# Coefficient matmuls taken apart and begun ahead of the first lookup, in a recommendation tower on one NeuronCore

## The reference

```python
e = jnp.stack([tbl_0[ids[:, 0]], ..., tbl_15[ids[:, 15]]], axis=1)     # (2048, 16, 16)
A = jnp.repeat(x0, s, axis=1)                                          # x0: (2048, 39, 16)
Bm = jnp.repeat(xl, f, axis=2).reshape(b, s * f, d)                    # xl = e
z = jnp.einsum('bnh,bnd,nk,khd,kd->bkh', A, Bm, alpha, w, hv[..., 0])
h = jnp.concatenate([z.reshape(B, -1), dense_ctx], axis=1)             # 256 + 16
h = jnp.maximum(h @ W_top1 + b_top1, 0.0)                              # 512
h = jnp.maximum(h @ W_top2 + b_top2, 0.0)                              # 256
y = h @ W_top3
```

## Time and profile before

| what | value |
|---|---|
| median of 3 runs | 206.78 us (206.12 to 207.69) |
| profiled execution | 207.17 us, of it 205.4 us span of the core |
| PE busy | 171.9 us, 84% of the span |
| DVE busy | 149.0 us, 73% |
| ACT busy | 65.1 us, 32% |
| POOL busy | 113.2 us, 55% |
| mean granted TensorE clock | 0.95 of 2.4 GHz |

### The profile page before, as it was taken

One profiled execution on the slowest core, in us unless ns is written; L12 is line 12 of the kernel. 1 busy time (PEld: TensorE's weight loads), 2 busy tenths in 40 slices (PEclk: granted clock), 3 DMA queues, 4 the chain that ended last, 5 costly groups with the idle time before them and its releaser, 6 DMA issues.

```text
span 205.4 us, 5054 instructions
## 1 busy us (share of the span) xinstructions
PE 171.9 (84%) x2170; PEld 128.2 (62%) x2170; DVE 149.0 (73%) x171; ACT 65.1 (32%) x203; POOL 113.2 (55%) x119
## 2 busy tenths in 40 slices
PE   0318958998638899999967999999899899899983
PEld 0307947896425677677845677777577467477671
DVE  3798872109999979898899968866979595595000
ACT  2098000729300118216201271181117317311322
POOL 2687777777777777777777777777750000000000
PEclk9999995558996999999999999999999999999999
DMA  6495999999837992991039819800693790000000
GB/s 199 146 305 156 218 205 201 271 181 267 214 77 143 197 207 27 214 199 21 6 70 199 164 26 229 175 13 10 155 206 65 184 222 6 0 3 0 3 0 2
DMA packets 11698, 26.63 MB, mean 130 GB/s; under 512 B 3836, under 2 KB 6396, under 8 KB 9628
## 3 DMA queue, kind: packets, MB, share of 16 engines
q1 hardware_dynamic: 5356, 20.50, 45.2%
q10 hardware_dynamic: 2688, 4.76, 7.7%
q0 software_dynamic: 3632, 1.06, 4.6%
HBM read 26.26 MB, written 0.05 MB: 128 GB/s over the span
## 4 chain that ended last, share of the span: by engine, by line
PE 59%; DVE 26%; issue 9%; DMA 2%; ACT 1%; SPq 1%; ACTq 0%; DVEq 0%
DVE prod L576 14%; PE bank L667 13%; PE bank L688 13%; PE bank L698 12%; PE bank L627 10%; PE bank L610 4%; DVE picked L536 4%; DVE onehot L524 3%; PE bank L682 2%; PE bank L657 2%; DMA prod<-slot_mask 2%; PE bank L608 2%; DVE dense_sb L466 1%; DVE prod L498 1%; PE bank L707 1%
## 5 line engine op out<-in xcount | busy, mean ns | idle before, releaser
L322 POOL DMA_INDIRECT e_all<-tbl,ids_sb x112 | 111.7, 998 | 37.6 <-issue 33.8
L576 DVE TENSOR_TENSOR prod<-x_main,bank 128x2048 f32<-128x2048 f32 x32 | 72.2, 2279 | 17.9 <-PE bank L657 9.1
L667 PE MATMUL bank<-prod,coef 128*32 128x256 f32 x640 | 43.5, 391 | 9.0 <-DVE prod L576 8.9
L627 PE MATMUL bank<-parts,onehot 125*128 125x80 bf16 (+1 forms) x864 | 39.6, 211 | 11.6 <-DVE onehot L524 5.6
L627 PEld LDWEIGHTS bank<-parts,onehot 125*128 125x128 bf16 x864 | 37.3, 108 | 15.8 <-issue 6.0
L401 ACT ACTIVATE spread<-e_all 128x128 f32<-128x128 f32 (+3 forms) x128 | 29.0, 329 | 17.5 <-DVE e_all L540 17.2
L667 PEld LDWEIGHTS bank<-prod,coef 128*32 128x32 f32 x640 | 17.0, 110 | 23.4 <-DVE prod L576 12.7
L688 PE MATMUL bank<-z_sb,w1z_sb 128*128 128x256 f32 x128 | 30.3, 380 | 0.0
L698 PE MATMUL bank<-h_sb,w_sb 128*128 128x256 f32 x128 | 29.8, 386 | 0.7 <-ACT h_sb L411 0.7
L698 PEld LDWEIGHTS bank<-h_sb,w_sb 128*128 128x128 f32 x128 | 23.7, 190 | 6.9 <-ACT h_sb L411 3.1
L536 DVE TENSOR_TENSOR picked<-bank,pick 128x320 f32<-128x320 f32 (+1 forms) x36 | 16.7, 465 | 15.2 <-PE bank L627 15.1
(11 more groups left out here) (41 smaller groups left out, 77.2 us busy)
## 6 DMA issues: line engine op xcount, KB each, us to landing
x_main<-x_m SPq DMA_DIRECT2D x16, 512.0 KB
x_last<-x_l SPq DMA_DIRECT2D x8, 1024.0 KB
low_h<-low_dram ACTq DMA_DIRECT2D x6, 768.0 KB, 8.7
e_all<-tbl,ids_sb POOLq DMA_INDIRECT x112
x_last<-dense_t SPq DMA_DIRECT2D x8, 128.0 KB
prod<-small_tables SPq DMA_DIRECT2D x1, 672.0 KB, 4.6
w1z_sb<-w1z SPq DMA_DIRECT2D x1, 512.0 KB, 14.3
w_sb<-w SPq DMA_DIRECT2D x1, 512.0 KB, 14.3
```

What stands on the lines that cost most here:

```text
L322: pool.indirect_dma_start(out=e_all[:, t * E + s * D:t * E + (s + 1) * D], out_offset=None, in_=tables[s], in_offset=bass.IndirectOffsetOn ...
L576: dve.tensor_tensor(prod[:, c, :, :], x0[:, p, :, :], value_bank(g, c // 2)[:, c % 2 * GB:(c % 2 + 1) * GB].unsqueeze(1).broadcast_to([P, ...
L627: last = pe.matmul(look_ps[i % 2][:, t * w:(t + 1) * w], onehot[:, n, c, at:at + P], parts[:, part, col:col + w], start=(t == 0 and c == 0 ...
L667: last = pe.matmul(z_ps[p][32 * q:32 * q + 32, a * GB:(a + 1) * GB], coef[:, c, 4 * a + q, :], prod[:, c, 4 * a + q, :], start=(c == 0 and ...
```

## The change

PE: `make_coef` is taken apart into `main_coef` (four matmuls, into `c_ps`) and `last_coef` (one matmul, into `c4_ps`). Eight `main_coef` are issued ahead of the first lookup, one behind each lookup from n = 1 on, and two `last_coef` behind each lookup from n = 3 on; the last four `last_coef` stand behind the last lookup. `c_done` now counts to 2.

DVE: `multiply_weights` moves ahead of `spread_alpha`, and `make_pick` behind it. `split_dense` moves from behind the third product of group 0 to in front of the first. SP: the inputs of the coefficients go first and the small tables last; `low_h` is loaded on SP's queue and not on ACT's, the second set of it behind `x0` of group 1; dense and `w1d` are loaded ahead of `x0` of group 0. ACT: `round_dense` goes in front of `spread_group(0, 0)`.

```diff
-COEF_FROM, DENSE_AT = 3, 2
+COEF_FROM = 3
...
             sp.dma_start(ids_i, ids_d).then_inc(digits_in, 16)
-            sp.dma_start(table_sb, small_tables).then_inc(table_in, 16)
             sp.dma_start(masks_sb[:, :], masks).then_inc(masks_in, 16)
+            sp.dma_start(w_hv_sb[:, :], w_hv.unsqueeze(0).broadcast_to([J, D, K * H + K])).then_inc(coef_in, 16)
             sp.dma_start(alpha_sb[:, :, :], alpha.rearrange("(c p) k -> p c k", p=P)).then_inc(prep_in, 16)
             sp.dma_start(mask_sb, slot_mask).then_inc(prep_in, 16)
-
-            sp.dma_start(w_hv_sb[:, :], w_hv.unsqueeze(0).broadcast_to([J, D, K * H + K])).then_inc(coef_in, 16)
+            sp.dma_start(table_sb, small_tables).then_inc(table_in, 16)
+
+            def load_low(a, n, count):
+
+                sp.dma_start(low_h[:, n:n + count, :], low_dram[n:n + count, a * HALF:(a + 1) * HALF].unsqueeze(0).broadcast_to(
+                    [P, count, HALF])).then_inc(low_in[n // 3], 16)
+
+            sp.wait_ge(low_stored, 16)
+            for n in range(0, NSMALL, 3):
+                load_low(0, n, 3)
...
-            load_x0(0, 0)
             for q in range(4):
...
                 sp.dma_start(w1d_f[rows, :], w1d).then_inc(dense_in, 16)
+            load_x0(0, 0)
...
-            for g in range(1, GROUPS):
+            load_x0(1, 1)
+            sp.wait_ge(onehot_ready, 2 * NSMALL)
+            for n in range(0, NSMALL, 3):
+                load_low(1, n, 3)
+            for g in range(2, GROUPS):
                 load_x0(g, g % 2)
...
-                act.wait_ge(c_done, 1)
+                act.wait_ge(c_done, 2)
...
-            act.wait_ge(low_stored, 16)
-            for n in range(0, NSMALL, 3):
-                load_low(0, n, 3)
             spread_weights()
             spread_sums()
...
+            round_dense()
             act.wait_ge(pads_done, 1)
             spread_group(0, 0)
             copy_coef()
-            round_dense()
-            act.wait_ge(onehot_ready, 2 * NSMALL)
-            for n in range(0, NSMALL, 3):
-                load_low(1, n, 3)
...
+            multiply_weights()
+            spread_alpha()
             make_pick()
-            spread_alpha()
...
-            multiply_weights()
             split_tables(1, slice(FIRST_COLS, W))
...
+            split_dense()
             for i in units_at(0):
...
                     if g == 0 and c == 3:
-                        dve.wait_ge(c_done, 1)
+                        dve.wait_ge(c_done, 2)
...
-                    if g == 0 and c == DENSE_AT:
-                        split_dense()
...
+            sum_alpha()
+            pe.wait_ge(bsum_copied, 2)
+            pe.wait_ge(wblock_done, 1)
+            for k in range(K - NSMALL + 1):
+                main_coef(k)
+            pe.wait_ge(split_step, 4)
             made = 0
-            sum_alpha()
-            pe.wait_ge(split_step, 4)
             for n in range(NSMALL):
                 if n == 3:
                     pe.wait_ge(split_step, 8)
                 look_up(n)
+                if n > 0:
+                    main_coef(K - NSMALL + n)
+                if n == COEF_FROM:
+                    pe.wait_ge(blast_done, 1)
                 if n >= COEF_FROM:
-                    make_coef(made)
-                    made += 1
+                    for k in range(made, made + 2):
+                        last_coef(k)
+                    made += 2
             for k in range(made, K):
-                make_coef(k)
+                last_coef(k)
```

More of the change, by code:

```diff
@@ L328, in _ @@
         def _(act):
-            def load_low(a, n, count):
-                act.dma_start(low_h[:, n:n + count, :], low_dram[n:n + count, a * HALF:(a + 1) * HALF].unsqueeze(0).broadcast_to(
-                    [P, count, HALF])).then_inc(low_in[n // 3], 16)
             act.wait_ge(warm_ready, 1)
@@ L597, in sum_alpha, with main_coef @@
                 last.then_inc(bsum_done, 1)
-            def make_coef(k):
-                if k == 0:
-                    pe.wait_ge(bsum_copied, 2)
-                    pe.wait_ge(wblock_done, 1)
-                    pe.wait_ge(blast_done, 1)
+            def main_coef(k):
                 for j in range(2):
@@ L607, in make_coef, with last_coef @@
                         row = 64 * j + 32 * odd
-                        pe.matmul(c_ps[row:row + FM, k * MC * HP:(k + 1) * MC * HP], bsum_sb[:, 0:FM, k],
-                                  wblock[:, k, j::2, odd::2], start=True, stop=True)
+                        last = pe.matmul(c_ps[row:row + FM, k * MC * HP:(k + 1) * MC * HP], bsum_sb[:, 0:FM, k],
+                                         wblock[:, k, j::2, odd::2], start=True, stop=True)
+                if k == K - 1:
+                    last.then_inc(c_done, 1)
+            def last_coef(k):
                 last = pe.matmul(c4_ps[:, k * H:(k + 1) * H], blast[:, k, :, :, :].rearrange("p h f j -> p (h f j)"),
```

## The result

The changed kernel takes 201.05 us (median of 4 runs, 198.93 to 202.37) where the one before takes 206.45 (206.08 to 207.69): a ratio of 0.969, 95% interval 0.960 to 0.979. Run once more on another occasion it gave 200.69 (198.22 to 206.03) and 0.965 (0.958 to 0.972).

A forecast was written before the change was run, and what follows sets the result against it. It took the path through PE's coefficients to the first product, then DVE and PE taking turns on the chain, as the bound; -3.9 - 3.8 - 0.3 + 1.2 - 1.9 + 0.3 = -8.4 from 206.78 gave 198.4 us, range 195.6 to 202.4.

The forecast's parts named there:

- The tail of coefficients: PE between last lookup and transposes: coefficients drop under ACT's spread, transposes start at about 40.7 instead of 44.54; gain 3.9.
- The dense split: DVE's split_dense, on the chain between third and fourth product, moves under ACT's spread and the transposes; gain 3.8 us.
- PE's half clock: First products of group 0: starting earlier, they meet PE still slow; cost 0.3, bounds 0 to 1 us.
- The start: Preparation before the first lookup: weight multiplication leaves the stretch between the table splits; -0.3, bounds -0.3 and +1.0.
- the coefficients between the lookups: PE's coefficient matmuls placed behind the lookups cost 0 to 1.5 us; taken as 1.2.
- The pause: PE's 3.23 us stop in lookup 7, read as a late instruction block; gain 0 to 3.4, taken as -1.9.
- rival 2: No pause at all, full clock kept: lookups gain about 1.9 more than in the sum, giving 196.5; chance 0.13.
- one of two blocks is at risk: Instruction block needed near matmul 347, in lookup 8, is asked for in the x0 flood; one pause probably remains; hence -1.9.
- What could hold it back: Transfers and gathers: x0 of group 0 lands at 38.4 to 40.65, before its use; group 2's gathers keep over 3 us.
- Rival 4: x0, gathers or the second low_h load hold a later group by 2 to 4 us: 200.4 to 202.4; chance 0.07.
- That a microsecond before group 2 is one of the total: A microsecond won before the end of group 0 is one of the total, unless transfers or gathers hold it back.

The follow-up runs named there:

- low_h-around-x0: Changed kernel with the first third of the second low_h set sent ahead of x0 of group 2, the rest behind it: 200.37 us, ratio 0.966.
- no-flood: Kernel before, with SP holding back x0 of group 0 and all behind it until lookup 7 had run: 214.06 us in one execution.
- coefficients only: Changed kernel with x0 ahead of dense, rounding and second low_h set on ACT behind copy_coef, split behind the third product: 203.59 us, ratio 0.976.
- tail late: Changed kernel with x_last of group 1, and low_h behind it, issued only when group 1 has been spread: 205.99 us, ratio 0.991.
- both: Changed kernel with x_last on its own semaphore, and x_last of group 1 and low_h behind the spread of group 1: 200.73 us, ratio 0.963.
- dense only: Kernel before with dense and w1d ahead of x0, rounding ahead of the first spread, split before the first product, coefficients untouched: 200.13 us, ratio 0.968.
- warm: Changed kernel with second low_h set split around x0 of group 2, x_last's own semaphore, ten identity transposes before the first lookup: 200.27 us, ratio 0.957.

## Why the prediction was right

The forecast was 198.4 us in a range of 195.6 to 202.4; 201.05 and 200.69 were measured. Sign and range held, and the gain is 5.4 to 6.5 us where 8.4 was forecast. Part of that is luck. The sum's terms ahead of the first product (-3.9 - 0.3 + 1.2 - 1.9) put it at 41.1, and it came at 40.73, but not by that path: the lookups ended 4.3 us earlier than forecast, with which the transposes allowed a product near 36.9, and the wait for x0 took it back. Two errors of opposite sign nearly cancelled. Point by point:

- **The tail of coefficients, 3.9.** Right in the mechanism: the transposes start when the spread ends (35.3 against 35.41), and PE is idle 3.19 us in front of them. But the dense part alone reached the same time with the tail in place. What the tail gives up, the landing of x0 behind the dense pieces takes: 40.73 with the short tail, 41.91 with the long one. Alone, without the dense pieces in front, the coefficient part is worth 2.4% (0.976, interval 0.972 to 0.981).
- **The dense split, 3.8.** Hidden as said, between 31.59 and 35.38. In the second profile the stretch of the five products shrank by 4.05 us, in the first by 2.83: there PE's half clock cost about 1.2, where the sum had 0.3, just beyond the bound of 1 that was given for it.
- **The start and the coefficients between the lookups, +0.9.** The first lookup began at 15.59, 0.26 late instead of 0.3 early; in the second profile at 16.52, 1.2 late, just beyond the bound of 1.0. At the fast rate the coefficients between lookups cost next to nothing: a lookup every 1.7 to 1.9 us, and every 1.5 to 1.7 before. At the slow rate they cost 0.4 us a lookup: 2.85 in the low_h-around-x0 profile, 2.43 in the no-flood one.
- **The pause, mis-sized: -1.9.** It left entirely. The ninth sum moved by 5.3 us instead of 1.0, as in rival 2. The reading of instruction blocks holds: no pause without the flood, none in the lookups behind the dense pieces with PE's order unchanged, one ahead of matmul 347 in the two kernels that were sending x0 when PE came to matmul 220, and a block's packet sent late beside each pause. What failed is the reason for "one of two blocks is at risk": in the changed kernel the second block was asked for not in the flood of x0 but among the dense pieces, and it was there 4.3 us early.
- **What could hold it back: this step failed.** It took x0 as a floor of 38.4 to 40.65, "2 to 4 us under my sum", with the product at about 42. Its own terms put the product at 41.1, which leaves 0.4 to 2.7. x0 came at 40.7, the upper end, and with the lookups early it was the bound. The prediction also counted 3 us of slack for the gathers from when they are issued, and passed over that their landing is not fixed: 5.4 us behind the last issue in the kernel before, 10.8 and 9.9 in the two profiles of the changed kernel, 8.3 to 10.2 in the others where the spread waited for them. With a gap in the transfers there (before, coefficients only, tail late, both) that spread started at 49.4 to 50.5, without one at 51.0 to 53.6; that the gap is the cause is likely from this and not shown, as the same program gave 50.96 and 53.55. The late gathers took back 1.7 us in the first profile; in the second x0 of group 2 took back 2.45. Rival 4 named this (2 to 4 us), with a chance of 0.07, too low.
- **That a microsecond before group 2 is one of the total** held: from group 2 to the end of the span all fourteen profiles show 121.4 to 122.5 us.

The rules of the Trainium skill that were weighed (Runtime: NRT & Kernel Launch, "Instruction fetch mechanics") fare so: blocks of 16 KiB agree with the 17 packets, and "mostly hidden" holds in the changed kernel, while 3.23 and 1.51 us were exposed in the two kernels that send x0 first, and 1.23 in dense only.

Why no variant goes below 199.5, each experiment shows in part: with fast lookups, x0 of group 0, the gathers of group 1 and x0 of group 2 stand in line, and removing one shows the next; with slow lookups, none of them holds a start unless the edit itself sends something later, and the first product starts at 43 to 44 anyway, 5 to 6 us later than it could. Both ways lead to group 2 at 75 to 77 where no edit pushed a transfer back. What stays open is what puts PE at one rate or the other: of the eleven profiles of kernels with the coefficients ahead of the lookups four had it slow throughout and a fifth (warm) from the third lookup on, those of the three kernels without them never throughout. Three are too few to call the coefficient matmuls the cause. It wasn't settled.

## What to carry to other kernels

When a stage is cut from two sides at once, make each half alone: here the dense part by itself was worth all of it. Work moved out of the way of a transfer-bound stretch is repaid only up to the next transfer, and a landing time read from one trace is not a constant to reckon with: the same gather took from 5.4 to 10.8 us here. An unexplained stop in the middle of a run of independent matmuls is worth a count of instructions and a look at what the queues are sending, the queue of instructions above all.

## What the runs showed of the hardware

A pause of PE with no releaser stood at one of two places in the instruction count, 127 matmuls apart, and came and went with what was being sent: 3.23 us behind matmul 219 in the kernel before, 1.51 and 1.23 us behind matmul 346 in two kernels of different order. A 16 KB packet of queue 8 ends 1.4 to 1.7 us before PE goes on in all three. Everywhere else the packet had ended 2.3 us or more before PE came to either place, and there was no pause. The same 24 matmuls took 1.02 us in one execution and 1.76 in another, of kernels with the same PE order up to there, and the column of the granted clock reads 1.00 for both; the two stretches, of the changed kernel and of the one with low_h around x0:

```profile
22.00:30.00 8.00, 7.91 (x163) 7.37 (x164) 7.83 (x19) 1.03 (x2) 6.17 (x7) 1.00 0.79 195
```

```profile
22.00:38.00 16.00, 16.00 (x203) 14.92 (x200) 9.59 (x22) 2.53 (x3) 12.04 (x14) 1.00 0.93 204
```

That is 20 matmuls a microsecond in the first and 13 in the second. The first change of the clock that a trace records is in each case a rise: at 19.86 in the changed kernel, and at 44.59 in the one with low_h around x0, whose lookups were all slow by then. So the column shows 1.00 up to the first recorded change whatever the rate was, and there the rate is to be read from durations.
